# Centred rows stored by pairs of channels, written two neighbours at a time and read back with a step of two

## The chip, the cores and the metric

The program runs on one core of a Trainium2 chip. Its engines work side by side, each through its own list of instructions: TensorE (PE; its weight loads are shown apart as PEld), VectorE (DVE), ScalarE (ACT), GpSimd (POOL) and SyncE (SP), which only issues transfers here. They wait for one another through semaphores. The metric is the device time of one execution in microseconds (us); less is better.

## The reference, cut to what matters

```
x = x + attn(layernorm(x))      # x: 8 x 4096 x 512
x = x + ffn(layernorm(x))

def layernorm(x):
    m = mean(x, -1); v = var(x, -1)
    return (x - m) / sqrt(v + 1e-5)

def attn(x):                    # a long causal filter per channel, by FFT in the reference
    q = 1 - sigmoid(delta) * sigmoid(alpha)
    k[d, l] = sum_n p * beta * gamma * scale * q ** l     # 16 states per channel
    return irfft(rfft(x) * rfft(k))[:l] + x * omega
```

The second part sends each of 4096 tokens through two of eight low-rank experts (rank 64, inner width 2048, gelu) and adds the weighted results. All numbers are fp32.

## The kernel before

Of the eight sequences the kernel does four in a first half, then the experts' work, then the other four sequences (half 2). In the profiled execution the first half of the filter runs from about 132 to 416 us, the second from about 898 to 1184 us.

Within a half, the 512 channels are taken in four **tiles** of 128 channels. A tile of x lies in `xb`: 128 partitions (places within a chunk of 128 time steps), 128 rows (sequence and chunk) and 128 channels next to one another. There are two such buffers. While one tile is worked on, SyncE stores the tile before it and then loads the tile after it into the other buffer, in 16 pieces of 512 KB each; the first tile of a half has nothing to store, the last has nothing to load. No centring of a new tile starts before its 16 pieces are in (`wait(..., s_x, tiles_in(i, g))`).

A tile is worked off in 16 **units** of eight channels (`UC` is 8; unit u is half k of block i, so `u = 2i + k`). For each unit:

- The centring writes `cen = x - mean` in two halves: GpSimd (L509, in `centres`) does four channels, VectorE (L1123, `centre`) the other four. Each is an instruction of 128 partitions by 512 elements that goes row by row and, within a row, over four channels. It reads four neighbours of `xb` and the row's mean four times over. In `cen` the rows of one channel are neighbours, so each element is written 128 words away from the one before it.
- The scaling (L1134, `stage`, VectorE) writes `xn = cen * rstd` for all eight channels, 128 by 1024 elements, channel by channel; it reads `cen` and `rstd` in order and writes `xn` in order. TensorE reads `xn`.
- TensorE does `chunk` (L1319, what each chunk adds to the states), `between` (L1344, what the carried states give) and `local` (L1332, the filter within a chunk).
- ScalarE makes `carry` (L840) and `shift_s` (L844) and builds the filter matrices in `wb` (L863, L864, L870).
- VectorE runs the recurrence over the chunks (L1160, the scan, writes `state`) and adds TensorE's result to x in place (L1144, `add`).

VectorE's order for unit u is written out in its `steps`: scaling of unit u+1, centring of unit u+2, scan of unit u, add of unit u-1. GpSimd's centring of unit u+2 is allowed to start once the scan of unit u has ended (`wait(pool, s_st, u - 1)`), and the scaling of a unit waits for both centrings. After every second centring GpSimd copies decay factors into `near` (L479). In the first half it also issues small indirect transfers (L459).

`cen` and `xn` have two units' room each. Between and around the halves the same memory is used under other names (`par`, `load1a`, `act_h`), always as one flat row.

Of the kernel before, what the change touches and what calls it, by code (L numbers as in the profile page):

```python
# [20 lines left out]
P = 128  # L21
# [6 lines left out]
def wait(eng, sem, value):  # L28

    if isinstance(value, int) and value <= 0:  # L30
        return
    eng.wait_ge(sem, value)  # L32
# [16 lines left out]
def build(nc, x, delta, alpha, beta, gamma, omega, ew, ei, w1a, w1b, w2a, w2b, out, ei_experts=8):  # L49
# [7 lines left out]
    UC = P // N  # L57
# [8 lines left out]
    QB = UC // 2  # L66
# [41 lines left out]
    with ctx:  # L108
        def sb(name, shape, dt=F32):
            return ctx.enter_context(nc.sbuf_tensor(name, shape, dt))  # L110
# [14 lines left out]
        near = sb("near", [P, 2, SB, 3, N])  # L125
        dk = sb("dk", [P, WB, N * KD])
        wide = sb("wide", [P, 2 * UC * P])
        cen = sb("cen", [P, 2, UC, P])
        xn = sb("xn", [P, 2, UC, P])
        far = sb("far", [P, CR + P])  # L130
        half = sb("half", [P, 2])
# [4 lines left out]
        mean = sb("mean", [P, R])  # L136
        var = sb("var", [P, R])
        rstd = sb("rstd", [P, R])
# [8 lines left out]
        spare = sb("spare", [P, 4])  # L147


        cen_row = cen[:].rearrange("p k d r -> p (k d r)")  # L150
        xn_row = xn[:].rearrange("p k d r -> p (k d r)")
        par = cen_row[0:NU, 0:8 * P].rearrange("p (a b) -> p a b", a=8)
        zero = xn_row[:, D + 2 * NQ * E:D + 2 * NQ * E + 4 * ZR].rearrange("p (a z) -> p a z", a=2)
# [171 lines left out]
        def tile_half(g, i):  # L325
            return (i // BT + g) % 2
# [3 lines left out]
        def unit_view(eng, g, i, k):  # L330

            row = tile_half(g, i) * P
            col = (i % BT) * KD + k * UC
            if not isinstance(i, int):
                row, col = eng.snap(row), eng.snap(col)
            return xb_row[:, bass.ds(row, P), bass.ds(col, UC)]
# [45 lines left out]
        def tiles_in(i, g):  # L382

            return ((i - g * BT) // BT) * 16 * PIECES

        @block.gpsimd
        def _(pool):
# [65 lines left out]
            def send(c):  # L453

                if c == 0:
                    pool.wait_ge(s_rt, NROUTE)
                    pool.wait_ge(s_slot0, 16)
                wait(pool, s_scat[c % SQ], 16 * (c // SQ))
                pool.indirect_dma_start(  # L459
                    out=slot_d, out_offset=bass.IndirectOffsetOnAxis(ap=pos_col[:, c:c + 1], axis=0),  # L460
                    in_=row_col[:, 2 * c:2 * c + 2], in_offset=None,
                    bounds_check=SL - 1, oob_is_err=False).then_inc(s_scat[c % SQ], 16)

            def clear(h):

                pool.memset(wb[:, h, :, :, 0:2 * ZR], 0.0).then_inc(s_wz, 1)
# [6 lines left out]
            def place_decays(i):  # L473

                dst = near[:, i % 2][:, :, 0:3:2, :]
                src = dk[:, i % WB].rearrange("p (n s d) -> p s d n", s=SB, d=2)
                wait(pool, s_loc, 2 * (i - 1))
                wait(pool, s_dk[i % WB], 16 * (i // WB + 1))
                pool.tensor_copy(dst, src).then_inc(s_wd, 1)  # L479

            def scatter(q, k):

                at = q * 2 if isinstance(q, int) else pool.snap(q * 2)
                for h in range(2):
                    wait(pool, s_s[2 * (1 - k) + h], 16 * ((q + 1) // 2))
                pool.tensor_copy(pick_s[:, 2 * k:2 * k + 2], slot_s[:, bass.ds(at, 2)]).then_inc(s_pk, 1)
                hold(pool, s_pk, q + 1, s_const)
                for h in range(2):
                    hold(pool, s_ys, 2 * q + h + 1, s_const)
                    pool.indirect_dma_start(  # L490
                        out=o_tok[0:T], out_offset=bass.IndirectOffsetOnAxis(ap=pick_s[:, 2 * k + h:2 * k + h + 1], axis=0),
                        in_=route_o[:, 1 - k, h, :], in_offset=None,
                        bounds_check=T - 1, oob_is_err=False, compute_op=ALU.add).then_inc(s_s[2 * k + h], 16)

            def tile_start(i, g):

                return isinstance(i, int) and i % BT == 0 and i != g * NK

            def centres(g):
                def centre(i, first, final):  # L500
                    for k in range(2):
                        u = 2 * i + k
                        if k == 0 and tile_start(i, g):
                            place_decays(i)
                        if not (g == 0 and isinstance(i, int) and i < BT):
                            wait(pool, s_x, tiles_in(i, g))
                        wait(pool, s_xn, u - 1)
                        wait(pool, s_st, u - 1)
                        pool.tensor_tensor(cen[:, k, 0:UC // 2].rearrange("p d r -> p r d"),  # L509
                                           unit_view(pool, g, i, k)[:, :, 0:UC // 2],  # L510
                                           mean[:, g * P:(g + 1) * P][:, :, None].to_broadcast([P, P, UC // 2]),
                                           ALU.subtract).then_inc(s_cen, 1)
                        if g == 1 and first and k == 0:
                            scatter(NQ - 1, 0)
                        if k == 0 and not tile_start(i, g) and not (g == 1 and first):
                            place_decays(i)
                        if g == 0 and first and k == 1:
                            clear(1)
                        if g == 0 and SENT + u < NSEND:
                            send(SENT + u)  # L520
                for i in range(g * NK, (g + 1) * NK):
                    centre(i, i == g * NK, i == (g + 1) * NK - 1)
# [438 lines left out]
        def _(dve):  # L961
# [155 lines left out]
            def centre(g, i, k):  # L1117

                u = 2 * i + k
                if not (g == 0 and isinstance(i, int) and i < BT):  # L1120
                    wait(dve, s_x, tiles_in(i, g))
                wait(dve, s_xn, u - 1)
                dve.tensor_tensor(cen[:, k, UC // 2:].rearrange("p d r -> p r d"),  # L1123
                                  unit_view(dve, g, i, k)[:, :, UC // 2:],
                                  mean[:, g * P:(g + 1) * P][:, :, None].to_broadcast([P, P, UC // 2]),
                                  ALU.subtract).then_inc(s_cend, 1)

            def stage(g, i, k):

                u = 2 * i + k  # L1130
                wait(dve, s_loc, u - 1)
                wait(dve, s_cend, u + 1)
                wait(dve, s_cen, u + 1)
                dve.tensor_tensor(xn[:, k], cen[:, k],  # L1134
                                  rstd[:, g * P:(g + 1) * P][:, None, :].to_broadcast([P, UC, P]),
                                  ALU.mult).then_inc(s_xn, 1)

            def add(g, i, k):
# [8 lines left out]
            def steps(g, i, begin, end):  # L1147

                last = isinstance(i, int) and i == (g + 1) * NK - 1
                for k in range(2):  # L1150
                    u = 2 * i + k
                    if not (end and k == 1):
                        stage(g, i if k == 0 else i + 1, 1 - k)
                    if not end:
                        centre(g, i + 1, k)

                    wait(dve, s_sh, u + 1)
                    wait(dve, s_ca, u + 1)
                    wait(dve, s_pe, QB * (u - 1))
                    dve.tensor_tensor_scan(state[:, k, :], carry[:, k, CR:CR + P],  # L1160
                                           shift_s[:, k].rearrange("p b c -> p (b c)"), 0.0,
                                           ALU.mult, ALU.add).then_inc(s_st, 1)
                    if not (begin and k == 0):
                        add(g, i if k == 1 else i - 1, 1 - k)
                if end:
                    add(g, i, 1)
                    if not last:
                        centre(g, i + 1, 0)
                        stage(g, i + 1, 0)
                        centre(g, i + 1, 1)  # L1170

            dve.wait_ge(s_keep, NL)
            centre(0, 0, 0)
            stage(0, 0, 0)
            centre(0, 0, 1)
            over_tile_blocks(dve, 0, lambda i, begin, end: steps(0, i, begin, end))
# [323 lines left out]
```

## Time and profile before

| what | value |
|---|---|
| time, median of 3 runs | 1226.33 us (1225.64 to 1228.18) |
| time of the profiled execution | 1217.28 us |
| its span | 1215.3 us |
| busy: PE, DVE, ACT, POOL | 924.6, 914.0, 850.7, 628.5 us |
| mean TensorE clock, share of full speed | 0.93 |
| L1123, VectorE's centring | 128 times, 139.5 us |
| L509, GpSimd's centring | 128 times, 145.1 us |
| L1134, the scaling | 128 times, 176.4 us |

The median comes from other executions than the profiled one, which took 0.7% less. The span is the profiled execution without what lies around it (2 us). Busy times overlap between engines, so they don't add up to the span. A row of a timeline gives the start, the duration, the engine, the line, what is written from what, and in brackets how long the engine had been idle before and what ended that.

### The profile page before, as it was taken

The numbers are of one execution on the slowest core, as the hardware profiler recorded it, in microseconds if no ns is written. First come the engines' busy times: TensorE is split into PE (matmuls) and PEld (weight loads), VectorE is DVE, ScalarE is ACT, GpSimd is POOL, SyncE is SP. The second block draws the span as 40 slices with busy tenths as digits, with TensorE's granted clock in tenths as the row PEclk, the third lists the DMA queues.
The fourth block names the chain that finished last, engine by engine and source line by source line (L and its number), as shares of the span: only waits on it lengthen the run. The fifth ranks groups of instructions, "written<-read, shape, count | busy, mean of one in ns | idle before, by whom it ended". The sixth has DMA issues, their size and how long they took to land. (4 is left out here: it accounts for less than half of the span.)

```text
span 1215.3 us, 34118 instructions
## 1 busy us (share of the span) xinstructions
PE 924.6 (76%) x11452; PEld 747.5 (62%) x11452; DVE 914.0 (75%) x1495; ACT 850.7 (70%) x1191; POOL 628.5 (52%) x755
## 2 busy tenths in 40 slices
PE   4740587867868849899999999988988778587870
PEld 2530476756757737667777777766767667566760
DVE  6976898978979537777787787776549889697980
ACT  4852597977969736767677677676759889597970
POOL 4132686857855136666676766765663333232320
PEclk9985698998989979999999999999989999898995
DMA  6999684999999699999999888886359299999809
GB/s 235 338 400 327 178 195 121 287 265 296 263 280 319 202 282 294 270 253 238 272 218 228 238 223 218 235 212 141 90 135 236 64 290 268 292 272 277 245 2 274
DMA packets 337536, 287.89 MB, mean 237 GB/s; under 512 B 18088, under 2 KB 285000, under 8 KB 336962
## 3 DMA queue, kind: packets, MB, share of 16 engines
q1 hardware_dynamic: 292866, 211.22, 62.8%
q0 software_dynamic: 19520, 36.26, 15.1%
q10 hardware_dynamic: 25088, 39.60, 9.6%
q8 instruction: 37, 0.61, 0.2%
q14 instruction: 25, 0.20, 0.1%
HBM read 197.41 MB, written 100.61 MB: 245 GB/s over the span
## 5 line engine op out<-in xcount | busy, mean ns | idle before, releaser
L509 POOL TENSOR_TENSOR cen<-xb,mean 128x512 f32<-128x512 f32 x128 | 145.1, 1135 | 264.5 <-DVE state L1160 176.9
L1332 PE MATMUL ps<-xn,wb 128*128 128x128 f32 x2048 | 276.6, 291 | 0.0
L1332 PEld LDWEIGHTS ps<-xn,wb 128*128 128x128 f32 x2048 | 251.8, 201 | 17.8 <-issue 3.7
L937 ACT ACTIVATE cen<-ps 128x1024 f32<-128x1024 f32 x156 | 155.4, 1022 | 131.2 <-PE ps L1426 131.1
L1319 PE MATMUL ps<-xn,near 128*32 128x128 f32 x2048 | 87.7, 291 | 178.5 <-DVE xn L1134 99.9
L1134 DVE TENSOR_TENSOR xn<-cen,rstd 128x1024 f32<-128x1024 f32 x128 | 176.4, 1378 | 49.8 <-POOL cen L509 43.6
L1426 PE MATMUL ps<-carry,wb 64*128 64x256 f32 x1248 | 166.4, 395 | 26.7 <-DVE carry L1207 26.5
L1319 PEld LDWEIGHTS ps<-xn,near 128*32 128x32 f32 x2048 | 52.6, 113 | 201.6 <-issue 103.5
L1439 PE MATMUL ps<-cen,xn 128*64 128x128 f32 x2496 | 160.9, 276 | 1.4 <-ACT cen L937 1.3
L1144 DVE TENSOR_TENSOR xb<-xb,ps 128x1024 f32 (+1 forms) x128 | 152.9, 1194 | 10.1 <-PE ps L1344 10.1
L1439 PEld LDWEIGHTS ps<-cen,xn 128*64 128x64 f32 x2496 | 136.4, 137 | 38.6 <-ACT cen L937 31.6
L863 ACT ACTIVATE wb<-wide 32x1024 f32<-32x1024 f32 x128 | 146.4, 1144 | 16.6 <-DMA wide<-taps_d 13.9
L490 POOL DMA_INDIRECT out<-carry,pick_s x78 | 126.5, 1621 | 55.9 <-issue 50.5
L1123 DVE TENSOR_TENSOR cen<-xb,mean 128x512 f32<-128x512 f32 x128 | 139.5, 1090 | 13.5 <-DMA xb<-L_attn_x 13.4
L1426 PEld LDWEIGHTS ps<-carry,wb 64*128 64x128 f32 x1248 | 111.6, 186 | 56.4 <-issue 44.2
L1188 DVE BATCH_NORM_STATS2 tstat<-wide 128x6 f32<-128x512 f32 x78 | 53.8, 692 | 85.5 <-DMA wide<-y_d,pick_g 85.4
L864 ACT ACTIVATE wb<-wide 32x768 f32<-32x768 f32 x128 | 116.3, 908 | 1.5
L459 POOL DMA_INDIRECT slot_d<-rowf,posi x64 | 106.1, 1658 | 10.7 <-issue 9.8
L538 POOL DMA_INDIRECT wide<-y_d,pick_g x78 | 84.7, 1085 | 48.1 <-POOL pick_g L535 36.1
L555 POOL COPY xn<-xb 128x256 f32 x156 | 84.4, 571 | 48.1 <-PE ps L1439 47.3
L844 ACT ACTIVATE shift_s<-ps,coef 128x124 f32<-128x124 f32 x128 | 46.5, 363 | 86.2 <-PE ps L1319 83.5
L1344 PE MATMUL ps<-state,carry 32*128 32x128 f32 x2048 | 94.7, 300 | 0.1
(164 smaller groups left out, 1356.9 us busy)
## 6 DMA issues: line engine op xcount, KB each, us to landing
out<-xb SPq DMA_DIRECT2D x116, 512.0 KB, 6.0
xb<-L_attn_x SPq DMA_DIRECT2D x96, 512.0 KB
xb<-L_attn_x SPq DMA_DIRECT2D x32, 1024.0 KB, 9.9
xb<-L_attn_x ACTq DMA_DIRECT2D x128, 256.0 KB, 3.7
wb<-L_ffn_w_B SPq DMA_DIRECT2D x78, 256.0 KB
wide<-taps_d SPq DMA_DIRECT2D x60, 256.0 KB, 6.2
y_d<-xb SPq DMA_DIRECT2D x16, 512.0 KB, 6.3
dk<-decay_d SPq DMA_DIRECT2D x60, 128.0 KB, 5.1
```

The costliest lines, as they stand in the source:

```text
L490: pool.indirect_dma_start(out=o_tok[0:T], out_offset=bass.IndirectOffsetOnAxis(ap=pick_s[:, 2 * k + h:2 * k + h + 1], axis=0), in_=route_o ...
L509: pool.tensor_tensor(cen[:, k, 0:UC // 2].rearrange("p d r -> p r d"), unit_view(pool, g, i, k)[:, :, 0:UC // 2], mean[:, g * P:(g + 1) * ...
L863: act.activation(dst[0:ZR], src, ACT.Copy)
L864: act.activation(dst[ZR:2 * ZR, :, :, ZR:P], src[:, :, :, 0:P - ZR], ACT.Copy).then_inc(s_rev, 1)
L937: act.activation(act_h[:, b % 2].rearrange("p f t -> p (f t)"), ps[:, 2 * (b % 2):2 * (b % 2) + 2, :].rearrange("p a t -> p (a t)"), ACT.G ...
L1123: dve.tensor_tensor(cen[:, k, UC // 2:].rearrange("p d r -> p r d"), unit_view(dve, g, i, k)[:, :, UC // 2:], mean[:, g * P:(g + 1) * P][: ...
L1134: dve.tensor_tensor(xn[:, k], cen[:, k], rstd[:, g * P:(g + 1) * P][:, None, :].to_broadcast([P, UC, P]), ALU.mult).then_inc(s_xn, 1)
L1144: dve.tensor_tensor(view, view, ps[:, QB * k:QB * k + QB, 0:2 * P] .rearrange("p b (d r) -> p r b d", d=2), ALU.add).then_inc(s_ev, 1)
L1319: ins = pe.matmul(ps[b * 2 * N:(b + 1) * 2 * N, QB * k, 2 * P:3 * P], near[:, h, k * QB + b, d:d + 2, :].rearrange("p z n -> p (z n)"), xn ...
L1332: ins = pe.matmul(ps[:, QB * k + b, d * P:(d + 1) * P], wb[:, h, k * QB + b, d, :], xn[:, k, 2 * b + d, :], start=(b > 0 and d == 0), stop ...
L1426: ins = pe.matmul(ps[:, 2 * (b % 2) + h, f * QT:(f + 1) * QT].rearrange("p (a t) -> p a t", a=2), w1bs[half_rows, k, c * P:(c + 1) * P], r ...
L1439: ins = pe.matmul(ps[h * RANK:(h + 1) * RANK, 4, 0:P], w2as[:, (f // 2) * (FC // 2) + 2 * b + f % 2, :], act_h[:, b % 2, f, h * P:(h + 1) ...
```

## The change

`cen` gets the shape pair of channels, row, channel within the pair, in place of channel, row. So the two channels of a pair lie side by side in each row. Both centrings go over the same elements in the same order as before: row by row, four channels. They now write two neighbours, then jump 256 words to the next pair's two. The scaling still goes channel by channel and still writes `xn` in order, but reads `cen` with a step of two words. `rstd` is read as before. Number, order and waits of all instructions are the same on every engine; the size of `cen` is too.

```diff
-        cen = sb("cen", [P, 2, UC, P])
+        cen = sb("cen", [P, 2, QB, P, 2])
...
-        cen_row = cen[:].rearrange("p k d r -> p (k d r)")
+        cen_row = cen[:].rearrange("p k b r d -> p (k b r d)")
...
-                        pool.tensor_tensor(cen[:, k, 0:UC // 2].rearrange("p d r -> p r d"),
-                                           unit_view(pool, g, i, k)[:, :, 0:UC // 2],
-                                           mean[:, g * P:(g + 1) * P][:, :, None].to_broadcast([P, P, UC // 2]),
+                        pool.tensor_tensor(cen[:, k, 0:QB // 2].rearrange("p b r d -> p r b d"),
+                                           unit_view(pool, g, i, k)[:, :, 0:UC // 2]
+                                           .rearrange("p r (b d) -> p r b d", d=2),
+                                           mean[:, g * P:(g + 1) * P][:, :, None, None]
+                                           .to_broadcast([P, P, QB // 2, 2]),
                                            ALU.subtract).then_inc(s_cen, 1)
...
-                dve.tensor_tensor(cen[:, k, UC // 2:].rearrange("p d r -> p r d"),
-                                  unit_view(dve, g, i, k)[:, :, UC // 2:],
-                                  mean[:, g * P:(g + 1) * P][:, :, None].to_broadcast([P, P, UC // 2]),
+                dve.tensor_tensor(cen[:, k, QB // 2:].rearrange("p b r d -> p r b d"),
+                                  unit_view(dve, g, i, k)[:, :, UC // 2:].rearrange("p r (b d) -> p r b d", d=2),
+                                  mean[:, g * P:(g + 1) * P][:, :, None, None].to_broadcast([P, P, QB // 2, 2]),
                                   ALU.subtract).then_inc(s_cend, 1)
...
-                dve.tensor_tensor(xn[:, k], cen[:, k],
-                                  rstd[:, g * P:(g + 1) * P][:, None, :].to_broadcast([P, UC, P]),
+                dve.tensor_tensor(xn[:, k].rearrange("p (b d) r -> p b d r", d=2),
+                                  cen[:, k].rearrange("p b r d -> p b d r"),
+                                  rstd[:, g * P:(g + 1) * P][:, None, None, :].to_broadcast([P, QB, 2, P]),
                                   ALU.mult).then_inc(s_xn, 1)
```

## Rows read from the trace of the kernel before

**Rows 1.** Windows, one per tile of half 1: busy time (instructions), clock, DMA share, GB/s.
```profile
138.00:206.00 68.00, 54.42 (x763) 46.25 (x762) 59.50 (x65) 57.24 (x81) 49.38 (x41) 0.95 0.67 164
206.00:281.00 75.00, 55.69 (x774) 47.31 (x773) 60.69 (x65) 58.59 (x81) 51.38 (x40) 0.91 1.07 278
281.00:354.00 73.00, 56.17 (x773) 47.88 (x773) 61.48 (x66) 58.66 (x82) 50.59 (x40) 0.92 1.10 276
354.00:412.00 58.00, 48.35 (x708) 40.73 (x708) 51.59 (x57) 50.13 (x71) 30.84 (x27) 0.98 0.86 273
```
**Rows 2.** Timeline of DVE within a tile: start, duration, line.
```profile
299.89 1.54 DVE L1134 TENSOR_TENSOR xn<-cen,rstd 128x1024 f32<-128x1024 f32 x1 [0.27 <-POOL cen L509]
301.36 1.06 DVE L1123 TENSOR_TENSOR cen<-xb,mean 128x512 f32<-128x512 f32 x1
302.26 0.40 DVE L1160 TENSOR_TENSOR_SCAN state<-carry,shift_s 128x128 f32<-128x128 f32 x1
302.57 1.19 DVE L1144 TENSOR_TENSOR xb<-xb,ps 128x1024 f32 x1
304.03 1.23 DVE L1134 TENSOR_TENSOR xn<-cen,rstd 128x1024 f32<-128x1024 f32 x1 [0.27 <-POOL cen L509]
...
306.10 0.39 DVE L1160 TENSOR_TENSOR_SCAN state<-carry,shift_s 128x128 f32<-128x128 f32 x1
```
**Rows 3.** Timeline of POOL in the same stretch.
```profile
299.74 0.61 POOL L479 COPY near<-dk 128x256 f32<-128x256 f32 x1
...
302.84 1.09 POOL L509 TENSOR_TENSOR cen<-xb,mean 128x512 f32<-128x512 f32 x1 [0.52 <-DVE state L1160]
```
**Rows 4.** The three changed lines: ns of one, min/median/max, over the whole span.
```profile
L1123 DVE TENSOR_TENSOR cen<-xb,mean x128: 1029/1062/2054, 131.7 to 1172.7; 128x512 f32<-128x512 f32 x128
...
L509 POOL TENSOR_TENSOR cen<-xb,mean x128: 1091/1102/1836, 130.3 to 1174.1; 128x512 f32<-128x512 f32 x128
...
L1134 DVE TENSOR_TENSOR xn<-cen,rstd x128: 1202/1252/1996, 132.9 to 1175.4; 128x1024 f32<-128x1024 f32 x128
```
**Rows 5.** Lines of VectorE with two inputs and other steps, same columns.
```profile
L1063 DVE TENSOR_TENSOR carry<-idf,carry x2: 425/426/426, 14.2 to 14.7; 128x256 f32<-128x256 f32 x2
...
L1064 DVE TENSOR_TENSOR carry<-carry x1: 424/424/424, 15.1 to 15.1; 128x256 f32<-128x256 f32 x1
...
L1080 DVE TENSOR_TENSOR carry<-carry,small x1: 425/425/425, 29.2 to 29.2; 128x256 f32<-128x256 f32 x1
...
L1011 DVE TENSOR_TENSOR mean<-wb x1: 383/383/383, 127.4 to 127.4; 128x128 f32<-128x128 f32 x1
...
L1014 DVE TENSOR_TENSOR rstd<-rstd x2: 293/293/293, 128.5 to 830.3; 128x128 f32<-128x128 f32 x2
```
**Rows 6.** Lines of POOL with one input, same columns.
```profile
L451 POOL COPY xb<-xb x32: 607/616/897, 12.0 to 124.8; 128x512 f32<-128x512 f32 x32
...
L547 POOL COPY dk<-wb x39: 393/408/706, 434.1 to 878.9; 128x256 f32 x39
```
**Rows 7.** Timelines of ACT and PE at a tile's end, where neither is kept waiting.
```profile
195.91 0.62 ACT L840 ACTIVATE carry<-far,rate 128x384 f32<-128x384 f32 x1
...
199.42 0.61 ACT L840 ACTIVATE carry<-far,rate 128x384 f32<-128x384 f32 x1
...
195.52 0.64 PE L1319 MATMUL ps<-xn,near 128*32 128x128 f32 x16 [0.15 <-DVE xb L1144]
...
198.73 0.73 PE L1344 MATMUL ps<-state,carry 32*128 32x128 f32 x16
```
**Rows 8.** Timeline of DVE: a step after a start, and two changes of tile.
```profile
148.75 1.23 DVE L1134 TENSOR_TENSOR xn<-cen,rstd 128x1024 f32<-128x1024 f32 x1 [1.29 <-PE ps L1332]
...
200.74 1.03 DVE L1123 TENSOR_TENSOR cen<-xb,mean 128x512 f32<-128x512 f32 x1
...
274.23 1.04 DVE L1123 TENSOR_TENSOR cen<-xb,mean 128x512 f32<-128x512 f32 x1 [5.60 <-DMA xb<-L_attn_x]
```
**Rows 9.** Idle time of DVE before L1123 over the span, and what ended it.
```profile
  DMA xb<-L_attn_x: 13.4, 4
```

## The prediction

> **What bounds the kernel now.** I read the table of windows by tile first, then the timelines of VectorE and GpSimd inside a tile, then the durations of the changed lines, and last the instructions elsewhere that read or write memory in a like way.
>
> The windows show two kinds of tile [rows 1]. Tiles 2 and 3 of a half last 75 and 73 us with a DMA share of 1.07 and 1.10: they store one tile and load another, and the transfer engines never rest. Tiles 1 and 4 last 68 and 58 us at a share of 0.67 and 0.86. The change from tile to tile says the same: into tile 2 VectorE centres right behind its last add, with no idle time, while into tile 3 it waits 5.60 us for the tile's last piece [rows 8]. Over the span such waits come to 13.4 us in four places [rows 9], the ends of tiles 2 and 3 in both halves. So in four of eight tiles the work on the engines sets the time, in the other four the transfers do, and there a quicker VectorE only waits longer.
>
> Within a tile VectorE is the slowest. Its round for one unit is scaling, centring, scan, add [rows 2]. From one scaling to the next, 299.89 to 304.03, are 4.14 us; from one scan to the next, 302.26 to 306.10, are 3.84; the two kinds alternate, 3.99 on average. The only idle time is 0.27 us before the scaling, for GpSimd's centring: that starts at 302.84, after the scan has ended, takes 1.09 and so ends at 303.93 [rows 3]. The longer round is one in which the scaling takes 1.54 rather than 1.23 us; GpSimd's copy L479 starts just ahead of it, at 299.74. What the others need when nothing keeps them waiting shows at a tile's end [rows 7]: ScalarE goes from one `carry` to the next in 199.42 - 195.91 = 3.51 us, TensorE from `chunk` to the next unit's `between` without a chunk in 198.73 - 195.52 = 3.21 us.
>
> **VectorE's centring.** It takes 1062 ns for 512 elements [rows 4]. Instructions with two inputs in memory read in order take 293 ns for 128 elements (L1014) and 424 for 256 (L1064), 1.03 ns an element [rows 5]; so 512 would take 424 + 256 x 1.03 = 688 ns. The centring is 374 ns above that, 0.73 ns an element. L1011 reads both inputs with a step of six words and costs 383 - 293 = 90 ns more than L1014, 0.70 ns an element: an element away from its neighbour costs just this. In the centring it must be the written side: x is read in fours, and a mean that is repeated costs nothing (L1080 repeats a value 32 times over and takes 425 ns, as L1064 does). After the change every written element has a neighbour. The bounds are 688 ns (no price for pairs) and 1062 (no gain); at one price per pair it would be 688 + 256 x 0.73 = 875. I take 690, since the price in the rows belongs to elements that stand alone. Gain: 0.37 us a centring.
>
> **The scaling.** It now reads one input with a step of two words. L1063 does that: it compares the experts' numbers, which lie in pairs, reading one of each pair, 256 elements, and takes 425 ns against 424 in order [rows 5]. So the price is 0 ns, within 1 ns in 256. The other bound is L1011's 0.70 ns an element, which would be 0.72 us on 1024. I take 0, and keep the other end.
>
> The Trainium skill speaks on both sides here. Its Vector Engine (DVE) Microarchitecture Reference, § 5.2 Measured stream behaviour on trn2, says that a port runs at full rate only over runs of at least two adjacent words; by that the pairs written are free, and the scaling, whose step of two leaves no adjacent words, would cost 1.73 ns in place of 1.05 an element, about 0.7 us more. Its SBUF — State Buffer, § Door 1: The DMA port swizzle, says that two hits in a line of 16 bytes suffice, and by that a step of two is free. L1063's 425 ns agrees with the second page and speaks against the first; the first remains as a rival.
>
> **GpSimd's centring.** It takes 1102 ns [rows 4]. GpSimd's copies take 408 ns for 256 elements and 616 for 512 [rows 6], 0.81 an element and 200 fixed. Two inputs at that rate are 200 + 2 x 512 x 0.81 = 1030 ns, nearly what it takes now. So its reads set the time and the written step hides beneath; the reads stay the same. No GpSimd instruction in the trace writes or reads in runs of two. The bounds: down to the copy's 616, up by half of its price again (one more pass of 0.81 an element, 415 ns) to 1520. I take 1100, by the nearest row, the instruction itself. The 0.27 us of waiting then stay.
>
> **The sum.** The centring stands on VectorE's path in each round: the scan starts 0.90 us after it does now (301.36 to 302.26) and 0.53 after. The rounds become 3.47 and 3.77 us, 3.62 on average. That is above ScalarE's 3.51 and TensorE's 3.21, so both still keep up, though only just; the scan's input `shift_s` is ready long before.
>
> - A tile has 13 rounds with a centring between its first scan and its last stretch. Four tiles that are not bound by transfers: 4 x 13 x 0.37 = 19.2 us.
> - After each start TensorE is late once: at 148.75 the scaling waits 1.29 us for L1332 [rows 8]. In such a round VectorE's gain is lost, and about another third of a round while TensorE catches up: 4 x 0.5 = 2.0 us off.
> - Before a tile's first scan stand three centrings. Where they stand on the path (start of each half, start of tile 4 in each), they give at most 1.1 us each, and part goes to TensorE and ScalarE, which start cold; I put in 0.65 for each of the four: 2.6 us.
> - Tiles 2 and 3: 0. The work there gets some 5 us shorter and the waits of 5.60 us and the like get as much longer, since the transfers start with the end of tile 1 and are not slower or quicker for it.
>
> Together 19.2 - 2.0 + 2.6 = 19.8 us, from 1217.28 to 1197.5 us in the profiled execution's terms. The median of the runs is 9 us above that execution; taken off the median: 1226.33 - 19.8, about 1206 us.
>
> **The rivals.**
>
> 1. Half a gain. Pairs still pay one price each on VectorE (875 ns), or GpSimd gets slower by some 0.15 us, which its centring hands on in full, since the scaling waits for it. The round gains about 0.2: 4 x 13 x 0.2 + 1 = 11 us, 1215 us. For it: no row shows runs of two words being written. Against: a price per lone element fits the 0.73 so well.
> 2. More. Either GpSimd's centring falls too, the 0.27 of waiting goes and ScalarE's 3.51 sets the round, another 4 x 13 x 0.11 = 6 us (1200 us), or the transfers in tiles 2 and 3 turn out to follow the engines and these four tiles gain 4 x (13 x 0.37 - 0.5) = 17 us (1189 us). Against the second: a share over 1 throughout.
> 3. Slower, by the scaling's read. If a step of two costs what a step of six does, the round loses 0.72 and gains 0.37, 0.35 more. The free tiles and their two scalings at each start lose 4 x (13 x 0.35 + 0.4) = 20 us, the bound tiles the same less the 13.4 us that they wait now, 6 us: 1252 us. It decides from the point where the step costs over 0.37 us on 1024 elements, 0.36 ns each. Against it stands L1063 with 0.004.
> 4. No change or barely slower, by GpSimd: 0.4 us more on its centring, say because runs of two cost its loop more, pushes the scaling back by 0.4 and eats the 0.37: 0.03 to 0.07 a round, 1228 to 1230 us.
>
> **How the numbers follow.** Forecast 0.63, half a gain 0.12, more 0.10, slower by the read 0.07, by GpSimd 0.08. A difference of 0.2% (2.5 us) is about what a measurement of this kernel tells from none. The first three are faster by more: 0.85. Of the fourth and fifth, 0.10 is slower and 0.05 within 0.2%. The forecast's own spread is 1200 to 1212 us; reaching over the half gain and into the better cases, and leaving out rivals 3 and 4, the range is 1193 to 1224.
>
> **What would show it.** L1123 near 690 ns, L509 still near 1100, L1134 unchanged at 1.23 and 1.54; scans 3.47 and 3.77 us apart; tile 1 of half 1 shorter by 5 us, tile 4 by 5, tiles 2 and 3 of nearly the old length, with DMA waits before L1123 risen from 13.4 to some 30 us in all. L1134 near 1.9 us would prove the forecast wrong, and so would L509 at 1.4 or more; tiles 2 and 3 five us shorter would show that I misread the transfers.

## The result, and the profile after

The kernel after takes 1209.36 us (median of 4 runs, 1206.38 to 1210.82), the kernel before 1226.93 (4 runs, one more than above, 1225.64 to 1228.18). The medians lie 17.6 us, or 1.4%, apart. The ratio on record is 0.9845, which is not the quotient of the two medians (0.9857), with a 95% interval of 0.9824 to 0.9866: after is faster by 16 to 22 us. The profiled execution of after took 1210.82 us with a span of 1208.9.

The three changed lines over the whole span, ns of one as minimum, median and maximum. They answer to [rows 4]; the line numbers have moved by two.

```profile
L1125 DVE TENSOR_TENSOR cen<-xb,mean x128: 673/684/1711, 131.9 to 1166.5; 128x512 f32<-128x512 f32 x128
...
L509 POOL TENSOR_TENSOR cen<-xb,mean x128: 1084/1096/1657, 130.5 to 1167.7; 128x512 f32<-128x512 f32 x128
...
L1136 DVE TENSOR_TENSOR xn<-cen,rstd x128: 1208/1258/2000, 132.8 to 1168.9; 128x1024 f32<-128x1024 f32 x128
```

VectorE's centring went from 1062 to 684 ns. The other two moved by 6 ns each. The timeline of VectorE within a tile, to be laid beside [rows 2]:

```profile
298.83 1.55 DVE L1136 TENSOR_TENSOR xn<-cen,rstd 128x1024 f32<-128x1024 f32 x1 [0.27 <-POOL cen L509]
300.31 0.68 DVE L1125 TENSOR_TENSOR cen<-xb,mean 128x512 f32<-128x512 f32 x1
300.91 0.41 DVE L1163 TENSOR_TENSOR_SCAN state<-carry,shift_s 128x128 f32<-128x128 f32 x1
301.24 1.19 DVE L1147 TENSOR_TENSOR xb<-xb,ps 128x1024 f32 x1
302.70 1.23 DVE L1136 TENSOR_TENSOR xn<-cen,rstd 128x1024 f32<-128x1024 f32 x1 [0.26 <-POOL cen L509]
303.84 0.69 DVE L1125 TENSOR_TENSOR cen<-xb,mean 128x512 f32<-128x512 f32 x1
304.44 0.42 DVE L1163 TENSOR_TENSOR_SCAN state<-carry,shift_s 128x128 f32<-128x128 f32 x1
```

From scan to scan are 304.44 - 300.91 = 3.53 us, and 3.87 from scaling to scaling in the longer round, against 3.84 and 4.14. VectorE still waits 0.27 us for GpSimd, and the longer round still has the scaling of 1.55 us. The windows of half 1, tile by tile, beside [rows 1]:

```profile
137.00:200.00 63.00, 52.99 (x768) 45.14 (x768) 54.87 (x65) 56.88 (x81) 50.55 (x41) 0.99 0.76 177
200.00:275.00 75.00, 55.52 (x774) 47.40 (x774) 56.50 (x66) 58.44 (x82) 50.84 (x40) 0.89 1.12 282
275.00:348.00 73.00, 55.17 (x771) 46.81 (x770) 56.17 (x65) 57.53 (x81) 50.84 (x40) 0.90 1.12 272
348.00:402.00 54.00, 48.12 (x710) 40.84 (x709) 47.66 (x57) 50.01 (x72) 30.74 (x27) 0.99 0.94 297
```

Tiles 1 and 4 are shorter, 63 and 54 us instead of 68 and 58. Tiles 2 and 3 still last 75 and 73, at a DMA share of 1.12 in both. What VectorE saves there it spends waiting: into tile 3 now 9.11 us instead of the 5.60 of [rows 8], and over the span 34.9 instead of the 13.4 of [rows 9].

```profile
268.43 0.69 DVE L1125 TENSOR_TENSOR cen<-xb,mean 128x512 f32<-128x512 f32 x1 [9.11 <-DMA xb<-L_attn_x]
...
  DMA xb<-L_attn_x: 34.9, 4
```

One profiled execution is a thin basis for a difference of 1.4%: this pair differs by only 6.4 us of span. So each kernel was profiled twice more (below). The stretches of all six, in us, a tile being taken from its first scan to the next tile's first scan (tile 4: to its own last scan):

| stretch | before (three traces) | after (three traces) | gain of means |
|---|---|---|---|
| start to first scan | 138.0, 138.4, 137.5 | 137.3, 136.6, 136.8 | 1.1 |
| half 1, tile 1 | 68.2, 68.1, 68.5 | 63.1, 63.0, 63.0 | 5.2 |
| half 1, tiles 2 and 3 | 147.5, 148.1, 148.4 | 147.3, 145.8, 145.0 | 1.9 |
| half 1, tile 4 | 58.0, 57.9, 57.9 | 54.2, 54.2, 54.2 | 3.7 |
| experts | 497.5, 502.5, 506.8 | 505.4, 507.0, 505.0 | -3.5 |
| half 2, tile 1 | 67.5, 67.5, 67.5 | 63.1, 62.8, 62.8 | 4.6 |
| half 2, tiles 2 and 3 | 144.9, 144.9, 146.4 | 148.5, 145.5, 148.2 | -2.0 |
| half 2, tile 4 | 58.0, 57.9, 57.9 | 54.2, 54.2, 54.4 | 3.6 |
| last scan to end of span | 35.8, 35.8, 35.8 | 35.8, 35.8, 35.8 | 0.0 |
| whole span | 1215.3, 1221.1, 1226.7 | 1208.9, 1205.0, 1205.2 | 14.7 |

The tiles that the engines bound repeat to 0.4 us and gain 17.2 us together. The stretches with many transfers scatter by 1 to 9 us and gain nothing that can be told from that.

### The profile page after: what moved, and what is told of

Read it like the earlier page. It is cut to its first block and busy times, and to the rows that moved or that the text cites. A ratio compares the mean times of both kernels' runs of the same rounds, so it can differ in the third digit from the quotient of the medians.

```text
span 1208.9 us, 34118 instructions
## 1 busy us (share of the span) xinstructions
PE 926.7 (77%) x11452; PEld 748.2 (62%) x11452; DVE 874.9 (72%) x1495; ACT 843.8 (70%) x1191; POOL 621.3 (51%) x755
## 3 DMA queue, kind: packets, MB, share of 16 engines
q0 software_dynamic: 19520, 36.26, 15.1%
## 5 line engine op out<-in xcount | busy, mean ns | idle before, releaser
L1335 PEld LDWEIGHTS ps<-xn,wb 128*128 128x128 f32 x2048 | 251.4, 200 | 17.2 <-issue 2.7
L1429 PE MATMUL ps<-carry,wb 64*128 64x256 f32 x1248 | 170.8, 404 | 27.7 <-DVE carry L1210 27.1
L1442 PEld LDWEIGHTS ps<-cen,xn 128*64 128x64 f32 x2496 | 136.8, 137 | 38.3 <-issue 22.8
L1429 PEld LDWEIGHTS ps<-carry,wb 64*128 64x128 f32 x1248 | 114.3, 190 | 58.6 <-issue 46.2
L1125 DVE TENSOR_TENSOR cen<-xb,mean 128x512 f32<-128x512 f32 x128 | 91.3, 713 | 35.0 <-DMA xb<-L_attn_x 34.9
```

The lines of the kernel that those rows point to most:

```text
L1335: ins = pe.matmul(ps[:, QB * k + b, d * P:(d + 1) * P], wb[:, h, k * QB + b, d, :], xn[:, k, 2 * b + d, :], start=(b > 0 and d == 0), stop ...
L1429: ins = pe.matmul(ps[:, 2 * (b % 2) + h, f * QT:(f + 1) * QT].rearrange("p (a t) -> p a t", a=2), w1bs[half_rows, k, c * P:(c + 1) * P], r ...
L1442: ins = pe.matmul(ps[h * RANK:(h + 1) * RANK, 4, 0:P], w2as[:, (f // 2) * (FC // 2) + 2 * b + f % 2, :], act_h[:, b % 2, f, h * P:(h + 1) ...
```

## The experiments

"Before" beside each ratio was run on the same chip as the kernel it is compared with.

**Which of the two centrings?** In `dve_only` only VectorE's half of `cen` is laid by pairs and GpSimd writes as before. The scaling reads `cen` from end to end, so there is no step in it and the channels of that half are left in mixed order.

```diff
-                        pool.tensor_tensor(cen[:, k, 0:QB // 2].rearrange("p b r d -> p r b d"),
...
+                        pool.tensor_tensor(cen[:, k, 0:QB // 2].rearrange("p b r d -> p (b r d)").rearrange("p (c r) -> p r c", r=P),
...
-                dve.tensor_tensor(xn[:, k].rearrange("p (b d) r -> p b d r", d=2),
-                                  cen[:, k].rearrange("p b r d -> p b d r"),
...
+                dve.tensor_tensor(xn[:, k], cen[:, k].rearrange("p b r d -> p (b r d)").rearrange("p (c r) -> p c r", r=P),
```

> Only VectorE's half of cen is laid by pairs; GpSimd writes its half as before, and the scaling reads cen from one end to the other in order, so that xn gets VectorE's four channels in mixed order (the unmixing is left out). My theory: VectorE's centring alone carries the gain, so L1123's counterpart takes 684 ns, GpSimd's stays at 1102, the scaling at 1252 (no step at all), rounds 3.53 and 3.86 us, the time within 2 us of after (1207 to 1211). Rival, GpSimd's pairs carry part of it by taking the port for less time: rounds 3.6 or more, time 1213 to 1220.

Measured: 1203.46 us, ratio 0.9804 (0.9748 to 0.9861), an interval that reaches over after's. The time lies some 4 us under the 1207 to 1211 that were expected, with two of its four runs at 1200 and two at 1206 to 1208; why is open. The rounds are as expected, 3.54 and 3.86 us.

```profile
L1123 DVE TENSOR_TENSOR cen<-xb,mean x128: 677/684/1702, 131.0 to 1162.2; 128x512 f32<-128x512 f32 x128
...
L509 POOL TENSOR_TENSOR cen<-xb,mean x128: 1092/1104/1668, 129.6 to 1163.3; 128x512 f32<-128x512 f32 x128
...
L1134 DVE TENSOR_TENSOR xn<-cen,rstd x128: 1209/1276/1996, 131.8 to 1164.6; 128x1024 f32<-128x1024 f32 x128
```

`pool_only` is the mirror image: GpSimd's half by pairs, VectorE's as before, the scaling in order again.

```diff
-                dve.tensor_tensor(cen[:, k, QB // 2:].rearrange("p b r d -> p r b d"),
...
+                dve.tensor_tensor(cen[:, k, QB // 2:].rearrange("p b r d -> p (b r d)").rearrange("p (c r) -> p r c", r=P),
```

> Only GpSimd's half of cen is laid by pairs; VectorE writes its half as before and the scaling reads in order, so xn gets GpSimd's four channels in mixed order. My theory: nothing is gained: VectorE's centring 1062 ns, GpSimd's 1090 to 1102, rounds 3.82 and 4.14 us, time 1225 to 1229. Rival, the pairs help GpSimd or what waits for it: its centring under 1080 ns or rounds shorter by 0.05 us and more, time 1215 to 1223.

Measured: 1222.78 us, ratio 0.9975 (0.995 to 1.0), rounds 3.82 and 4.15 us, GpSimd's centring 1093 ns, VectorE's 1061. The time falls into the rival's range of 1215 to 1223, but the rounds and the centring don't, and the unchanged kernel before, run again on the same chip (`before_again`, below), took 1223.51: 0.7 us more.

VectorE's pairs alone give the whole gain, GpSimd's next to none: 9 ns of 1102. And the shortest scaling that reads in order (1209 ns in `dve_only`, 1202 in before) is shorter by at most 6 ns than the one with a step of two (1208).

**Where does a step begin to cost?** `fours` lays `cen` by fours of channels and computes the same. Its edit is shown against the kernel before. Both centrings write in order from end to end, the scaling reads with a step of four words.

```diff
-        cen = sb("cen", [P, 2, UC, P])
+        cen = sb("cen", [P, 2, 2, P, UC // 2])
...
-                dve.tensor_tensor(cen[:, k, UC // 2:].rearrange("p d r -> p r d"),
+                dve.tensor_tensor(cen[:, k, 1],
...
-                dve.tensor_tensor(xn[:, k], cen[:, k],
-                                  rstd[:, g * P:(g + 1) * P][:, None, :].to_broadcast([P, UC, P]),
+                dve.tensor_tensor(xn[:, k].rearrange("p (b d) r -> p b d r", b=2),
+                                  cen[:, k].rearrange("p b r d -> p b d r"),
+                                  rstd[:, g * P:(g + 1) * P][:, None, None, :].to_broadcast([P, 2, UC // 2, P]),
```

> cen laid by fours of channels: each centring writes in order from end to end of its half, and the scaling reads with a step of four words (16 bytes). It computes the same. My theory that a lone element costs 0.73 ns and a pair nothing: the centring stays at 684 ns or falls by under 10. For the scaling I have no row between a step of two (free) and of six (0.7 ns): if lines of 16 bytes decide (two elements needed in each), a step of four costs 0.7 ns on each of 1024 elements, the scaling takes 1.97 us, rounds about 4.25 and 4.6 us, time 1235 to 1260. If the step decides only beyond four words, it takes 1.26 us and the time is that of after.

Measured: 1265.54 us, ratio 1.0298 (1.024 to 1.0356), rounds 4.33 and 4.59 us. That is 5 us above the top of the range expected if a step of four pays.

```profile
L1123 DVE TENSOR_TENSOR cen<-xb,mean x128: 655/678/2256, 131.7 to 1221.6; 128x512 f32<-128x512 f32 x128
...
L1134 DVE TENSOR_TENSOR xn<-cen,rstd x128: 1955/2052/2668, 132.5 to 1224.0; 128x1024 f32<-128x1024 f32 x128
```

Runs of four and more instead of two take only 6 ns off the centring (678 against 684). The scaling's shortest goes from 1208 to 1955 ns, 0.73 ns for each of 1024 elements, the same price that a lone element had in the centring. So a step of 8 bytes is free to within 6 ns of 1024 elements, and one of 16 bytes pays in full. With the scaling this slow the tiles that transfers bound before are bound by VectorE too: its centring waits for a transfer once in the span, for 0.2 us.

**Does it take a neighbour, or an aligned one?** `odd` is the kernel after with `cen` moved by one word.

```diff
-        cen = sb("cen", [P, 2, QB, P, 2])
+        cen_raw = sb("cen_raw", [P, 2 * UC * P + 2])
+        cen = cen_raw[:, 1:2 * UC * P + 1].rearrange("p (k b r d) -> p k b r d", k=2, b=QB, d=2)
```

> The kernel after with cen shifted by one word of 4 bytes, so that every pair begins on an odd word: still two neighbours, but a pair in four lies across a border of 16 bytes... (a border lies between the two words of every other pair). It computes the same. If only the neighbour counts, the centring stays at 684 ns and the time at 1209. If aligned blocks of 8 bytes decide, each word stands alone and the centring is back at 1062 ns (1226 us); if lines of 16 bytes decide, half the pairs are split and it takes about 870 ns (1217 us). The scaling then reads one word in 8 bytes as before, so it stays at 1258 ns by the line theory, since each line still gives two.

Measured: 1213.68 us, ratio 0.9882 (0.9829 to 0.9935).

```profile
L1126 DVE TENSOR_TENSOR cen_raw<-xb,mean x128: 829/846/1840, 132.2 to 1166.8; 128x512 f32<-128x512 f32 x128
...
L1137 DVE TENSOR_TENSOR xn<-cen_raw,rstd x128: 1204/1278/2001, 133.2 to 1169.4; 128x1024 f32<-128x1024 f32 x128
...
300.63 0.39 DVE L1164 TENSOR_TENSOR_SCAN state<-carry,shift_s 128x128 f32<-128x128 f32 x1
...
304.60 0.39 DVE L1164 TENSOR_TENSOR_SCAN state<-carry,shift_s 128x128 f32<-128x128 f32 x1
```

The centring takes 846 ns, near the middle between 684 and 1062, and the longer round, here from scan to scan, is 3.97 us. If blocks of 16 bytes are what counts, every second odd pair lies inside a block and is free, and every other is split across a border and pays for both words: 684 + 256 x 0.73 = 871 ns, 25 more than measured. Were aligned blocks of 8 bytes what counts, it would be 1062. The time is 3 us under the 1217 that went with the 870 ns. The three readings (step two free, step four dear, odd pairs half dear) fit blocks of 16 bytes of which two words in succession must be used. The Trainium skill says in SBUF — State Buffer, § Door 1: The DMA port swizzle, that a line of 16 bytes must be hit at least twice, and the runs agree; that one can stride by up to 4 fp32 words for free, as the same box says, is refuted by the step of four. The Trainium skill's Vector Engine (DVE) Microarchitecture Reference, § 5.2 Measured stream behaviour on trn2, gives 1.30 ns an element for odd pairs in both sources, and 1.71 to 1.76 where one side or both sources hop to a far word with every element. The written side here measured (846 - 684) / 512 + 1.03 = 1.35 and 0.73 + 1.03 = 1.76, close to both. The Trainium skill's wording there, that the words must be adjacent, is refuted by the step of two.

**Are tiles 2 and 3 bound by transfers?** Both kernels were run with smaller stores: of the 8 rows of a piece that goes to `out`, 2 are stored and 6 are left out. Issues, waits and the stores that the experts read are unchanged.

```diff
-                        dst = o_rows[:, bass.ds(row, PR), bass.ds(d0, P)]
+                        dst = o_rows[:, bass.ds(row, 2), bass.ds(d0, P)]
+                        sp.dma_start(dst, xb_row[:, bass.ds(r0, 2), :]).then_inc(s_put[j], 16)
+                        continue
```

> The kernel before, but stores to out move 2 of each piece's 8 rows (six in eight rows of those pieces are never written; the issues, semaphores and the stores to y_d stay). It takes load off the transfer engines in tiles 2 and 3. My theory that these four tiles are bound by transfers: they fall from 75.3, 72.2, 74.6 and 70.3 us to about 67.7 each, the DMA waits before L1123's counterpart from 13.4 to under 1 us, the changes of tile from 17, 13, 16 and 12 us to 9.3; the time to about 1205. Rival, the changes of tile are long for another reason (TensorE starting cold): they stay over 12 us and the time over 1218.

> The kernel after with the same smaller stores (2 of 8 rows per piece of out). My theory: with no tile bound by transfers the new centring pays in all eight tiles, tiles 1 to 3 63.1 us and the last of a half 54.2, so the time is 3 x 4.6 + 3.8 = 17.6 us per half and 35 in all under that of before with small stores, about 1170, twice the 17.6 us between the full kernels. Rival, the four middle tiles gain little even so, since another engine takes over: 18 to 22 us under it, 1185.

Measured: before with small stores 1181.08 us, ratio to before 0.9624 (0.9569 to 0.9679); after with small stores 1146.78 us, ratio 0.9339 (0.9282 to 0.9396). The windows of tiles 1 to 4 of half 1, first of before, then of after:

```profile
137.00:205.00 68.00, 54.03 (x771) 46.12 (x771) 59.79 (x66) 58.15 (x81) 50.03 (x41) 0.98 0.68 166
205.00:273.00 68.00, 53.87 (x770) 45.91 (x770) 59.91 (x65) 57.74 (x80) 50.01 (x40) 0.98 0.92 224
273.00:341.00 68.00, 53.92 (x765) 45.71 (x765) 59.90 (x65) 57.39 (x81) 50.00 (x40) 0.95 0.92 225
341.00:399.00 58.00, 48.68 (x713) 41.40 (x711) 51.60 (x58) 51.26 (x72) 30.82 (x27) 0.99 0.63 206
```

```profile
136.00:199.00 63.00, 53.39 (x771) 45.54 (x771) 54.92 (x65) 56.93 (x81) 50.55 (x41) 0.99 0.73 177
199.00:263.00 64.00, 54.65 (x768) 46.27 (x767) 55.92 (x66) 57.63 (x81) 50.01 (x40) 0.95 1.02 242
263.00:326.00 63.00, 53.03 (x768) 45.19 (x768) 55.26 (x64) 56.98 (x81) 50.26 (x40) 0.99 1.01 243
326.00:381.00 55.00, 49.58 (x718) 42.24 (x717) 48.57 (x59) 51.20 (x73) 30.78 (x27) 0.98 0.68 222
```

With less to store all three early tiles have one length, 68 us in before and 63 to 64 in after, and neither kernel waits for a tile's pieces at L1123's counterpart any more. In before the four changes of tile that took 17, 13, 16 and 12 us now take 9.2 to 9.8, so the rival falls. Over all eight tiles this pair of traces differs by 33.8 us. The same edit is now worth 1181.08 - 1146.78 = 34.3 us, twice the 17.6 of the full kernels. The level of 1205 that was expected for the first of them was wrong by 24 us. Of these, 21 come from the last stores, which shrink as well: from the last scan to the end of the span are 14.6 us instead of 35.8. That part says nothing on the question.

**Can the longer round be shortened?** In every second round GpSimd's copy into `near` begins 0.15 us ahead of the scaling, which then takes 0.31 us more. `delay` puts a fill between GpSimd's centring and that copy.

```diff
+        junk = sb("junk", [P, 2 * P])
...
                         if k == 0 and not tile_start(i, g) and not (g == 1 and first):
+                            pool.memset(junk[:], 0.0)
                             place_decays(i)
```

> The kernel after with a fill of 256 elements of an unused tile (0.3 us) on GpSimd between its centring and its copy into near, so that the copy no longer begins 0.15 us ahead of VectorE's scaling, which costs the scaling 0.31 us in every second round. If the instruction that begins first keeps the memory to itself and the other waits at no cost to VectorE, rounds of 3.87 us become 3.55 and the time falls by 4 x 6 x 0.31 = 7 us to 1202. If the copy gets in between the scaling and the centring instead, it costs VectorE 0.3 to 0.6 us there: rounds of 3.85 to 4.1, time 1208 to 1216.

Measured: 1216.48 us, ratio 0.99 (0.9873 to 0.9928). That is slower than the kernel after, and 0.5 us above the expected 1208 to 1216. The timelines of VectorE and GpSimd in half 2:

```profile
1144.61 1.23 DVE L1138 TENSOR_TENSOR xn<-cen,rstd 128x1024 f32<-128x1024 f32 x1 [0.27 <-POOL cen L510]
1145.75 1.13 DVE L1127 TENSOR_TENSOR cen<-xb,mean 128x512 f32<-128x512 f32 x1
1146.80 0.41 DVE L1165 TENSOR_TENSOR_SCAN state<-carry,shift_s 128x128 f32<-128x128 f32 x1
...
1144.44 0.32 POOL L519 MEMSET junk<- 128x256 f32 x1
1144.70 1.62 POOL L480 COPY near<-dk 128x256 f32<-128x256 f32 x1
```

The scaling is back at 1.23 us, and the copy that began 0.09 us after it takes 1.62 us and not 0.62. But it gets in ahead of the centring, which takes 1.13 rather than 0.69. The round is 3.98 us, longer than the 3.87 it was to cure; in half 1, where the small transfers queue behind the copy, the other round grows as well, to 3.95. The second case of the expectation holds. None of the variants that compute the reference is quicker than the kernel after.

**How much does one execution say?** Both kernels were profiled again.

> The kernel before, unchanged, profiled once more. The profiled execution of before took 1217.28 us, 9 us under its median, that of after 1210.82, at the top of its runs; 8 us of the missing difference lie in the experts' stretch, where no changed line runs. If that is variation from one execution to the next, this execution takes 1224 to 1229 us and its experts' stretch (last scan of half 1 to first scan of half 2) about 505 us instead of 497.5, the four tiles not bound by transfers staying at 68.2, 58.0, 67.5 and 58.0 us. If the change itself slows the experts' stretch (rival), the stretch stays at 497 to 499 us here.

> The kernel after, unchanged, profiled again. In six traces with a centring of VectorE at 846 ns or more the experts' stretch took 497.5 to 502.5 us, in those with 690 or less 503.6 to 506.8 (one trace each). If that is chance, this one and the two runs beside it fall anywhere between 497 and 507 without regard to the kernel. If a quicker first half makes the experts' stretch longer (rival), the after kernels are at 503.5 to 507 again and before at 497.5 to 502.5, and the change loses some 5 us there of the 14.7 us that the halves gain.

> The kernel after once more, the same question: between 497 and 507 us if it is chance, 503.5 to 507 if the change lengthens the experts' stretch.

> The kernel before once more: anywhere between 497 and 507 us in the experts' stretch if it is chance, 497.5 to 502.5 if only the change lengthens it.

The profiled copy of before took 1223.07 us with an experts' stretch of 502.5, halfway between the two cases of its expectation, and its other stretches repeat. Medians on their chips: 1223.51 us for the copy of before (ratio 0.9982, 0.9948 to 1.0015), 1206.86 for the copy of after (0.9838, 0.9746 to 0.993), and single times of 1207.25 and 1228.51 for the last two. In the spans shown in the table above, before lies anywhere between 1215.3 and 1226.7 us, 9.3 of these 11.4 us in the experts' stretch. The first three traces had suggested that the change lengthens that stretch, 505.4 us against 497.5 and 502.5. The third of before took 506.8 there, with the old centring, so the claim that only the change does it falls.

Whether the mean moves stays open, but the experiments' traces lean that way. The stretch took 501.1 us in `pool_only`, 500.9 in `odd` and 498.6 in `before_fewst`, with a centring of 846 ns or more; it took 506.9 in `dve_only`, 506.1 in `fours`, 505.5 in `delay` and 503.6 in `after_fewst`, with one of 691 or less. With the three traces of each kernel the means are 501.2 us over six traces and 505.6 over seven, and only one trace, the 506.8, breaks the order. (The expectation for `after_again` speaks of six traces with the slow centring, up to then; there were five.) No run shows what in the experts' stretch would depend on the centring. If it does, 4 us of the gain in the halves are lost there.

## Why the prediction was right

1206 us was forecast, 1209.36 measured; 19.8 us of gain against 17.6.

- **VectorE's centring.** 690 ns forecast, 684 measured, and `dve_only` shows that it carries the gain alone. The price of a lone element, read from L1011 in quite another part of the kernel (0.70 ns), compares with (1062 - 684) / 512 = 0.74 here. The in-order slope was (424 - 293) / 128 = 1.02 ns and not 1.03, which moves the forecast by 2 ns.
- **The scaling.** No price for a step of two, taken from L1063 with 256 elements: it went up by 6 ns, in the median (1252 to 1258) and in the minimum (1202 to 1208), and `dve_only`, which reads in order, has 1276 and 1209. The rival (0.7 ns an element, 1252 us) is a real effect that is there at a step of four, as `fours` shows with 1265.54 us.
- **GpSimd.** Unchanged, as forecast; its wait of 0.27 us stayed. That its two reads hide the written step was argued from the copies' rates; `pool_only` shows only that the pairs don't help it.
- **The term that was mis-sized: 0.37 us a round.** It measured 0.29 (3.82 to 3.53). The gain of 374 ns was taken from durations, but VectorE's instructions overlap: in [rows 2] the scan starts 0.90 us after a centring of 1.06, and now 0.60 after one of 0.68. The overlap fell from 0.16 to 0.08 (and is 0.12 in `odd`, between the two), so only 0.30 reached the path. The prediction had the 0.90 in hand and took 0.37 off it without asking whether the overlap stays. 4 x 13 x 0.29 is 15.1 us in place of 19.2; from the first to the sixteenth scan the four tiles together became 15.0 us shorter in the means of three traces. For the same reason tile 4 of a half became shorter by 3.7 and 3.6 us, not the 5 named as a sign.
- **TensorE's late rounds, 2.0 us off.** The prediction read one such round and counted four. In all three traces of before it comes only after the start of half 1, a round of 4.84 to 4.89 us in place of 4.13; the other starts have none. There TensorE had idled (2.28 us in the second trace), and then ran at the lower of its two clock levels: the granted clock is 0.50 from 144.50 to 147.90. The three traces of after have no late round. In the first of them TensorE idles 1.33 us at that place and keeps a granted clock of 1.00 from 142.70 to 147.00. The rows are TensorE's timeline in the second trace of before and in after:

```profile
144.09 0.77 PE L1319 MATMUL ps<-xn,near 128*32 128x128 f32 x16 [2.28 <-DVE xb L1144]
144.79 1.24 PE L1344 MATMUL ps<-state,carry 32*128 32x128 f32 x16
145.96 2.96 PE L1332 MATMUL ps<-xn,wb 128*128 128x128 f32 x16
```

```profile
142.70 0.64 PE L1322 MATMUL ps<-xn,near 128*32 128x128 f32 x16 [1.33 <-DVE xb L1147]
143.27 0.73 PE L1347 MATMUL ps<-state,carry 32*128 32x128 f32 x16
143.93 2.05 PE L1335 MATMUL ps<-xn,wb 128*128 128x128 f32 x16
```

  That the change keeps the late round away is not shown. With the old centring it is missing there in `pool_only` and `before_fewst`, where TensorE idles 1.19 and 1.55 us and the round takes 4.12; `pool_only` has it in tile 4 instead (4.93 us). With the new centring `after_fewst` has it after the start of half 2 (4.68 us), behind an idle time of 1.63 us:

```profile
889.67 0.64 PE L1324 MATMUL ps<-xn,near 128*32 128x128 f32 x16 [1.63 <-DVE xb L1149]
890.25 0.73 PE L1349 MATMUL ps<-state,carry 32*128 32x128 f32 x16
890.90 3.45 PE L1337 MATMUL ps<-xn,wb 128*128 128x128 f32 x16
```

  What decides where it comes stays open. At the end of the same tile the last two rounds take 3.63 and 3.49 us in after and 2.98 and 3.39 in the first trace of before, where in after the scan waits 0.56 us for ScalarE's `shift_s`. That isn't the change either: the third trace of before has 3.59 and 3.49 with the same wait, and `dve_only` has 3.00 and 3.37.

- **The starts, 2.6 us.** From VectorE's first centring to the first scan are now 5.37 us instead of 6.38 at the start of half 1, 10.48 instead of 11.06 at that of half 2, and 6.40 and 6.21 instead of 7.28 and 7.12 at the two starts of tile 4: 3.4 us in all, the same to 0.03 us in all three traces. The two changes from tile 1 to tile 2 took 1.0 to 1.3 us less each as well, but that lies ahead of stretches that transfers bind.
- **Tiles 2 and 3 at nothing.** Right: +1.9 and -2.0 us, the waits up from 13.4 to 34.9 us (some 30 had been forecast; the other traces have 14.0 and 16.4 before, 30.3 and 32.9 after), and with the stores cut these tiles gain like the others.
- **The sum.** That 19.8 lies so near 17.6 is in part luck: the rounds were put 4 us too high, the late rounds took 2 us off for something that mostly isn't there, the starts were 0.8 too low, and the 3.5 us by which the experts' stretch was longer in the traces stood in no term. The interval of the ratio, 16 to 22 us, holds both numbers; that the rounds were mis-sized is shown by the traces and not by the time.

## What to carry to other kernels

Read the price of an access pattern from whatever instruction of the trace has it, in ns an element above one that reads and writes in order; it held here for a line in another stage. Take a gain per round from start to start on the engine, not from durations. Then ask in which stretches that engine sets the time: half of the tiles here were bound by transfers, and half of the gain went into a longer wait.

## What the runs showed of the hardware

- On VectorE in fp32 all runs fit one rule, that words which follow one another in time must hit a block of 16 bytes twice: a step of two words costs nothing (1208 ns against 1209 for 1024 elements), a step of four 0.73 ns an element (1955 ns), pairs beginning on odd words 0.32 (846 ns against 684 for 512). Reading with a step of four words (0.73 ns) and writing with one of 128 (0.74) have the same price. On GpSimd, which reads two inputs, pairs in place of lone written words are worth 6 to 10 ns of 1102 (1096 in after, 1093 in `pool_only`, 1092 for runs in order in `fours`).
- Of VectorE's scaling and GpSimd's copy, the one that begins later takes longer: the scaling 1.55 us instead of 1.23 when the copy began 0.15 us ahead, the copy 1.62 instead of 0.62 when the scaling began 0.09 us ahead. In the second case the copy ended first and VectorE's next instruction, the centring, took 1.13 us instead of 0.69.
- The same program differs from one execution to the next: 19 runs of before on one chip range from 1219.58 to 1233.78 us (1.2%). Between the three traces of before, 9.3 of 11.4 us lie in the experts' stretch.
- The clock granted to TensorE fell from 1.00 to 0.50 for 3.4 us behind an idle time of 2.28 us; `local` then took 2.96 us for the same work as 2.05.
